# Experts' stage: variance written behind the router, and the next-but-one group's normalisation at the end of ScalarE's order

## What is computed

```
h = _layernorm(x, axis=-1) * (1 + cb) + sb
scores = jnp.maximum((h @ gate_W + gate_b) / TEMP, EPS)      # 8 experts
p = jax.nn.softmax(scores, axis=-1)
...
w = jnp.maximum(p, W_THRES)                                  # the two best, weighed
comb = jnp.where(topk_mask, w / total, 0)
y = jnp.einsum('bsd,edf->bsef', h, expert_W) + expert_b
x = x + gb * jnp.einsum('bsef,bse->bsf', y, comb) / K
```

## Time and profile before

| | us |
|---|---|
| median of 3 runs | 3385.74 |
| lowest and highest run | 3384.83, 3385.99 |
| profiled execution, its own time | 3387.09 |
| its span in the trace | 3385.4 |
| TensorE busy in the span | 3242.3 |
| VectorE busy | 2475.3 |
| ScalarE busy | 1815.1 |
| GpSimd busy | 1433.2 |

### The profile page before, as it was taken

The page is one execution under the profiler, slowest core; times in us unless marked ns, Lnnn a source line. Parts: engine busy times, 40 slices in busy tenths (PEclk is TensorE's granted clock), DMA queues, the critical chain, the costliest instruction groups (busy, mean ns, idle before and its releaser), DMA issues. The chain is left out here.

```text
span 3385.4 us, 129353 instructions
## 1 busy us (share of the span) xinstructions
PE 3242.3 (96%) x51114; PEld 2751.5 (81%) x51114; DVE 2475.3 (73%) x6682; ACT 1815.1 (54%) x4493; POOL 1433.2 (42%) x1117
## 2 busy tenths in 40 slices
PE   6999999999999999999999999999968999999999
PEld 5888888888888888888888888888866877777777
DVE  5777777777777777776777777777647887877886
ACT  4666666666666666666666666666633222222221
POOL 3444445545544444454554444455431222222222
PEclk8999999999999999999999999999988999999999
DMA  4222222222222222222223222222221111111110
GB/s 142 78 78 74 77 78 80 79 75 75 85 86 78 77 80 73 78 78 78 75 80 92 78 76 81 78 78 72 72 67 63 39 38 51 39 39 39 51 38 26
DMA packets 158629, 238.74 MB, mean 71 GB/s; under 512 B 30232, under 2 KB 82504, under 8 KB 157768
## 3 DMA queue, kind: packets, MB, share of 16 engines
q1 hardware_dynamic: 158024, 230.33, 21.7%
HBM read 194.58 MB, written 35.67 MB: 68 GB/s over the span
## 5 line engine op out<-in xcount | busy, mean ns | idle before, releaser
L442 POOL TENSOR_TENSOR qs_sb<-lam_bc,qk_sb 128x512 f32<-128x512 f32 x256 | 531.4, 2076 | 1085.0 <-DVE qk_sb L925 950.6
L546 ACT ACTIVATE kd_sb<-bank_scores,decay 128x64 f32<-128x64 f32 x2048 | 446.1, 329 | 287.5 <-PE bank_scores L800 278.2
L908 DVE SCALAR_TENSOR_TENSOR s_mid<-s_mid,lam_bc,bank_dense 128x65 f32<-128x65 f32 x1536 | 433.8, 282 | 56.7 <-DVE s_mid L908 2.4
L450 POOL TENSOR_TENSOR oT_lo<-oT,oT_hi 128x512 fp32r<-128x512 f32 x256 | 327.6, 1280 | 81.8 <-ACT oT_hi L523 81.6
L505 ACT ACTIVATE qk_sb<-bank 128x512 f32<-128x512 f32 x512 | 316.7, 619 | 54.9 <-PE bank L585 36.9
L507 ACT ACTIVATE qk_sb<-qk_sb 128x512 f32<-128x512 f32 x512 | 323.3, 631 | 16.2
L960 DVE TENSOR_TENSOR p_sb<-bank_scores,decay 128x512 f32<-128x512 f32 x256 | 176.5, 690 | 204.7 <-ACT kd_sb L546 202.9
L583 PE MATMUL bank<-wv_hi,h_hi 128*128 128x256 f32 x1024 | 308.2, 301 | 12.9 <-DVE wv_lo L828 9.5
L931 DVE TENSOR_TENSOR_SCAN decay<-a_bc,eye 128x512 f32<-128x512 f32 x256 | 311.1, 1215 | 2.4 <-DMA a_bc<-rows_dram 2.2
L1286 DVE SCALAR_TENSOR_TENSOR acc<-bank,comb,acc 128x256 f32<-128x256 f32 x512 | 230.2, 476 | 103.1 <-ACT acc L1154 93.6
L800 PE MATMUL bank_scores<-qk_sb 64*64 64x128 f32 x8192 | 287.5, 276 | 9.3 <-ACT oT_hi L523 4.3
(11 more groups left out here) (199 smaller groups left out, 8627.1 us busy)
## 6 DMA issues: line engine op xcount, KB each, us to landing
a_bc<-rows_dram SPq DMA_DIRECT2D x512, 128.0 KB, 3.1
lam_bc<-rows_dram SPq DMA_DIRECT2D x512, 128.0 KB
x_in<-in_L_attn_x_dram SPq DMA_DIRECT2D x32, 512.0 KB, 5.9
x_res<-in_L_attn_x_dram SPq DMA_DIRECT2D x32, 512.0 KB, 4.0
x_dram<-x_res SPq DMA_DIRECT2D x32, 512.0 KB, 2.9
x<-x_dram SPq DMA_DIRECT2D x32, 512.0 KB, 3.3
out_dram<-x SPq DMA_DIRECT2D x32, 512.0 KB, 2.9
ew_raw<-in_L_ffn_expert_W_dram SPq DMA_DIRECT2D x8, 256.0 KB, 5.4
```

The lines of the kernel that those rows point to most:

```text
L442: pool.tensor_tensor(qs_sb[:, na, :], lam_bc[na][:, :], q_sb, ALU.mult).then_inc(qs_ready, 1)
L450: pool.tensor_tensor(oT_lo[:, u, :], oT32[:, :], oT_hi[:, u, :].bitcast(F32), ALU.subtract).then_inc(oT_lo_ready, 1)
L546: ins = act.activation(kd_sb[:, t, hd * DH:(hd + 1) * DH], KTR[:, hd, t * CK:(t + 1) * CK], ACT.Copy, scale=decay[:, hd, t, CK - 1:CK])
L908: dve.scalar_tensor_tensor(dst, src, lam_bc[nb][:, (ch + 1) * CK - 1:(ch + 1) * CK], U[ch], ALU.mult, ALU.add).then_inc(state_step, 1)
```

## The change

Two pieces of order are changed, and no operation is added or removed.

```diff
@@ ScalarE @@
             def group(T, s):
-                if exists(T + 1):
-                    ln_apply(T + 1, (s + 1) % GPB)
                 if exists(T):
...
+                if isinstance(T, int) and T == -2:
+                    ln_apply(0, 0)
                 if not exists(T + 1):
                     return
...
                     act.activation(eb[:, :], eb_raw[:, :], ACT.Copy).then_inc(eb_hi, 1)
+                if exists(T + 2):
+                    ln_apply(T + 2, (s + 2) % GPB)
                 act.wait_ge(combT_ps, Tn + 1)
...
@@ VectorE @@
                 if exists(T + 1):
                     route(T + 1, (s + 1) % 2, between)
+                    if exists(T + 2):
+                        ln_variance(T + 2)
                     adds(first + ROUTE - NCH, ADDS - BLOCK_ADDS)
                 else:
                     adds(first, ADDS - BLOCK_ADDS)
                     if exists(T + 2):
                         for ch in range(NCH):
                             ln_stats(T + 2, (s + 2) % GPB, ch)
-                if exists(T + 2):
-                    ln_variance(T + 2)
+                        ln_variance(T + 2)
                 adds(ADDS - BLOCK_ADDS, ADDS)
```

## The result

The changed kernel takes 3415.6 us (median of 4 runs, 3414.39 to 3417.03) against 3385.28 us: ratio 1.0091, 95% interval 1.0078 to 1.0103, so 30.3 us slower. Run again beside later experiments it gave 1.0097 (1.0082 to 1.0111). The forecast was 3413.4 us. Its mechanism is what the trace shows.

A forecast was written before the change was run, and what follows sets the result against it. Bound: the hand-offs from `shift` through `xn` to TensorE's transposes at each border. 23 x 0.89, 6 x 0.96 and 1.4 sum to 27.7 us on 3385.7: 3413.4 us, range 3405 to 3436.

The forecast's parts named there:

- The bound: At each border between groups TensorE waits for `xn` at the transposes, behind ScalarE's wait for `shift`: 29 times, 17.1 us.
- The variance moves nothing: VectorE: the variance is written ahead of an empty call for adds, so no instruction moves; price 0.
- The sum for one border: Delay of the transposes: 0.49 + 0.05 + 0.47 - 0.12 = 0.89 us in the loop, 0.96 in straight-line groups.
- Which borders: The delay counts at 23 loop and 6 straight-line borders; the loop's jump and the last border cost 0.
- The first group: At T = 0 the bias matmuls start at 2563.81 and the transposes come at 2564.74, 1.4 us later.
- What VectorE does with its surplus: VectorE's first addition comes 1.19 us later, 0.30 more than TensorE's delay; its 0.89 wait for TensorE swallows that.
- The clock rival: TensorE's longer wait before the bias matmuls lowers the clock, 1.59 us a border: 3450 or 3459.5 us; chance 0.16.
- The sign that I named for it: Granted clock of a loop stretch: 1.00 if the forecast holds, 0.9 if the clock rival is right.
- The point sum: All borders together: 20.5 in the loop, 5.8 in straight-line groups, 1.4 at the first group: 27.7 us, giving 3413.4.

The follow-up runs named there:

- e6: Changed kernel with statistics and variance of group T+2 moved to the very start of VectorE's group, into its wait for `acc`: 3361.76 us, ratio 0.993.
- e1: Changed kernel with `combT`'s copy put back ahead of the `xn` activations on ScalarE, rewritten variance kept: 3384.22 us, ratio 0.9999.
- e8: As e6, but with `combT` ahead of `xn` on ScalarE as in the kernel before: 3364.88 us, ratio 0.9939.
- e2: Changed kernel with `combT`'s copy between the second and the third `xn` activation: 3398.84 us, ratio 1.0046.
- e3: Changed kernel with `combT`'s copy behind the wait for `shift` but ahead of all four `xn` activations: 3400.12 us, ratio 1.005.
- e4: Changed kernel with one more activation of 128x256, its result unused, ahead of the four of `xn`: 3437.32 us, ratio 1.0162.

## Why the prediction was right, point by point

**The bound.** Right. One hand-off chain at each border (variance, `shift`, `xn`, transposes) set the period. e6, which takes it off the path, shortens the loop period by 0.82, which is the 0.61 and the 0.21 that TensorE waited at a border.

**The variance moves nothing.** Right: the orders were the same, and e1, which keeps the rewritten variance, gives 0.9999.

**The sum for one border.** The chain was right and its terms nearly so. Predicted delay 0.89 in the loop and 0.96 in straight-line groups; measured 0.92 (25.51 to 26.43) and 1.01 (25.20 to 26.21). The four bias matmuls took 0.48 from their start to the next weight load instead of 0.47 (2825.96 to 2826.44), and from the end of `combT` at 2825.91 to their start went 0.05, as taken. `combT` itself took 0.57.

**Which borders.** Right: 29 waits, the jump costs nothing (29.59 to 29.61). The first group was under-sized. Its transposes came 1.4 us later by the sum, and 2.16 later in the trace, counted from the last store of the attention half (35.91 to 38.07, with the transposes at 2563.32 and 2557.81). Of that 0.66 is an `xn` that ended later in this execution (35.86 us before, and 36.52 here by `combT`'s start at 2556.16, 0.10 ahead of the end of `xn`).

**What VectorE does with its surplus.** Right: its first addition came 1.18 later against the end of `shift` (predicted 1.19), it still waits 0.77 for block 1, and the period follows TensorE's delay. The wait was forecast to shrink by 0.3 and shrank from 0.89 to 0.77, by 0.12. Another 0.14 went one addition earlier: before, the first addition of block 1 came 1.72 us behind the first of block 0, as TensorE had its result no sooner, and now comes 1.58 behind it. The surplus was swallowed as forecast, but at two places.

**The clock rival.** I priced it at 23 or at 29 borders, gave that 0.16, and read the row with 1.43 us as a sign that 1.51 would hold. It was neither all nor none: the clock fell at 4 borders in one execution and at 2 in another. The price for one was right: 1.59 predicted, and 1.61 and 1.52 at the two borders that fell in the first execution and held in the second (28.12 against 26.51, 28.15 against 26.63). The sign that I named for it was too coarse: I would have read 0.9 over a loop stretch as the clock rival, and from 2675 to 2960 us, with two falls in it, the granted clock reads 0.99. The point sum left out these 3 to 6 us, and the range took them in.

**Why the number fitted.** 29.6 us for the change without falls, some 3 to 6 for falls, and an attention half that scatters by several us. Against the stage of the first profiles the sum of 27.7 is 8.4 short: 6.4 by falls, the rest by the terms above. The medians differ by 30.3, in the second comparison by 31.2 (its ratio of 1.0097 stands for 32.8); all are above 27.7. That the forecast lies only 2.2 us from the median is luck in so far as the stage grew by 32 to 36 us in the two profiles: the omitted falls and the under-sized terms were partly offset by an attention half that was shorter there. How many falls the executions without a profile had is not known.

## What to carry to other kernels

When two results of one engine are wanted in a certain order, write them in that order. A wait for a late input takes everything behind it along, here a copy whose input had long been there. Here whatever was put between that wait and the transposes was paid in full, with TensorE's own work between the two results on top; where the wait lay off the path (e6 against e8) the same order cost nothing. Before moving a step earlier in an order, check by the order of the built program that its input comes earlier too: a call over an empty range moved nothing here. What did make `shift` early was to put the statistics and the variance into an idle stretch of their engine, here VectorE's wait for `acc`; that gave 0.7%.

## What the runs showed of the hardware

In the changed kernel the granted clock fell behind waits of TensorE of 1.56 to 1.62 us at some borders and not behind waits of 1.73 and 1.74 in the same execution; with waits of 1.74 to 2.22 at 29 borders it fell at 6. At one and the same border, with the same wait, it fell in one execution and held in another. In these runs the length of the wait alone doesn't tell it. What else decides is open, no run here isolates it. In e2 and e3, where the waits from the second group on stayed at 1.31 us or less apart from the loop's jump, it fell at the jump alone. Even the jump's wait, 3.07 to 3.57 us in the twelve profiles, was followed by 1.2 GHz in eleven of them and not in e4, where it was 3.08. A fall cost 1.5 to 1.6 us, taken against the same place of the loop without one.

The first half of the kernel, with the same code, ended anywhere between 2519.7 and 2527.5 us in twelve profiles. A difference of a few us between two profiles has to be read stage by stage before it is given to a change. What makes the scatter was not looked into.
